# Gathering the x rows for a graph-and-gate kernel one layer earlier, through a DRAM copy in slot order

## The chip, the cores and the metric

The kernel runs on one core of a Trainium2 chip. The metric is the device time of one execution in microseconds; three runs were timed. A lower number is better.

## The reference

The input is x (10000 x 512, float32) and 10000 edges src -> dst, sorted by dst. What is computed, with every weight a 512 x 512 matrix:

```python
h = layernorm(x)
for l in range(3):
    h_neigh = segment_sum(h[src], dst, N) / max(deg, 1)
    rst = relu(h @ W_self[l] + h_neigh @ W_neigh[l] + b[l])
    h = rst / max(norm(rst), 1e-12)
x = x + h
xn = layernorm(layernorm(x)) # the inner one without, the outer one with gain and bias
# 8 experts of width 64; the two with the largest gate count, weighted by their softmax
x = x + layernorm(layernorm(x) + experts(xn)) # with out_g and out_b
```

So the last stage needs, for every node, its row of the input x beside its h of the third layer.

## The kernel before, in words

Edges are cut into T = 79 tiles of 127, and every node gets a slot in one of 79 x 128 = 10112 slots, so that a tile of 128 slots holds the nodes whose edges end there. `pinT` and `poutT` are tables of node numbers by slot. The program has four phases:

- Phase 0 walks over the nodes in natural order (79 tiles): layernorm, then two products (with W_neigh and W_self of layer 0), stored to DRAM as `y_rows0` and `self_rows0`. The weights are prepared and the tables built beside it.
- Phases 1 and 2 walk over the slot tiles. A step gathers the y rows of the edges (`gather`, L670), sums them by slot on TensorE (`aggregate`, L1639 and L1640), adds the node's own row (`combine`, L1295), normalizes (`sum_squares` L1303, `sum_floor` L1313, `norm` L695 on GpSimd, `hhi` L847, `hlo` L1319), turns the tile (L1599, L1172), multiplies it with both matrices of the next layer (`neigh` and `own`, 12 matmuls each, L454), and stores y (`put_y`, L702, an indirect DMA) and the own row (`store_self`, L541).
- Phase 3 aggregates the third layer and runs the residual, the gate and the experts. `x2` (L1338) adds the node's row of x, which `by_node` (L683), an indirect DMA of GpSimd, has gathered into `X[0]` or `X[1]`. `result` (L1499) makes the output tile and `put_out` (L756) scatters it.

Each engine runs its own list in order. `run_tiles` writes these lists: a stage with offset k works in step t on tile t + k. In phase 2 the list of GpSimd (POOL in the profile) for a step is gather(t+6), put_y(t), norm(t+3); that of SyncE (SP), which issues the plain DMAs, is store_self(t), load_self(t+5). In a step of phase 2 VectorE (DVE) does one_hot(t+5), hlo(t+2), ylo(t), turn(t+1), carry_lo, combine, sum_squares and sum_floor of t+3, and `sev` of t (L1189), for which SP's store waits. TensorE (PE) does neigh(t), turn(t+1), own(t), aggregate(t+3). Sl, X and SB are rings of two buffers, so that a load waits for the use of the tile two before, and `after(engine, sem, n)` is that wait.

In phase 1 `by_node` has the same place in the list of POOL and gathers the own rows into Sl; in phase 3 it stands between gather(t+7) and `xob` (L730, x2 plus the output bias, 128x512) and waits for the x2 of the tile before.

Of the kernel before, what the change touches and what calls it, by code (L numbers as in the profile page):

```python
# [14 lines left out]
P = 128  # L15
# [119 lines left out]
class SlotSems:  # L135


    def __init__(self, sem):
        self.g = [sem(f"g{i}") for i in range(GRING)]
        self.x = [sem(f"x{i}") for i in range(2)]  # L140
        self.xs = [sem(f"xs{i}") for i in range(2)]
        self.xg = [sem(f"xg{i}") for i in range(2)]
        self.ys = [sem(f"ys{i}") for i in range(2)]
        self.s2 = [sem(f"s2{i}") for i in range(2)]
        self.smat = sem("smat")
        self.c0 = sem("c0")
        self.chi = sem("chi")
        self.clo = sem("clo")
        self.agg = sem("agg")
        self.r = sem("r")  # L150
        self.rr = sem("relu")
        self.dv2 = sem("sumsq")
        self.ss = sem("sumsq_max")
        self.sc = sem("rnorm")
        self.hhi = sem("hhi")
        self.hlo = sem("hlo")
        self.tr = sem("turned")
        self.ht = sem("ht")
        self.y = sem("y")
        self.yhi = sem("yhi")  # L160
        self.ylo = sem("ylo")
        self.sp = sem("own")
        self.sev = sem("self")
# [54 lines left out]
def build(nc, x, src, dst, W_self, W_neigh, b, Wg, W1, b1, W2, b2, ln_g, ln_b, out_g, out_b, out):  # L218
    with ExitStack() as ctx:
# [9 lines left out]
        def dram(name, shape, dt):  # L229
            return nc.dram_tensor(name, shape, dt)  # L230
# [2 lines left out]
        Yd = [dram(f"y_rows{l}", [N, 2 * D], F16) for l in range(LAYERS)]  # L233
        Sd0 = dram("self_rows0", [N, D], F32)
        Sd = [None] + [dram(f"self_rows{l}", [SLOTS, D], F32) for l in (1, 2)]
        info = dram("node_info", [N, 2], F32)
        table = dram("slot_table", [SLOTS, 2], F32)

# [221 lines left out]
        @block.sync  # L460
        def _(sp):

            sp.wait_ge(s_epad, 3)
            full = (E // EPT) * EPT
            for to, frm, count in ((eDi, dst, E), (eSi, src, E), (eNi, dst[1:E], E - 1)):
                sp.dma_start(to[0:T - 1, :], frm[0:full].rearrange("(t k) -> t k", k=EPT)).then_inc(s_eload, 16)
                sp.dma_start(to[T - 1:T, 0:count - full], frm[full:count].rearrange("(a k) -> a k", a=1)
                             ).then_inc(s_eload, 16)

            sp.wait_ge(s_infoz, 2)  # L470
            sp.dma_start(info.rearrange("(p k) two -> p (k two)", p=NP_), zero).then_inc(s_tinit, 16)
            sp.dma_start(table.rearrange("(p k) two -> p k two", p=T), tinit).then_inc(s_tinit, 16)

            sp.dma_start(bcol[:, :], ln_b.rearrange("(c p) -> p c", p=P)).then_inc(s_bload, 16)
            sp.dma_start(gcol[:, :], ln_g.rearrange("(c p) -> p c", p=P)).then_inc(s_bload, 16)
            for l in range(LAYERS):
                sp.dma_start(bias[:, l, :], b[l, :].partition_broadcast(P)).then_inc(s_bload, 16)
            sp.dma_start(b1b[:, :], b1.rearrange("e h -> (e h)").partition_broadcast(P)).then_inc(s_bload, 16)
            sp.dma_start(ogb[:, :], out_g.partition_broadcast(P)).then_inc(s_bload, 16)
            sp.dma_start(obb[:, :], out_b.partition_broadcast(P)).then_inc(s_bload, 16)  # L480
            sp.dma_start(wgr[:, :, :], Wg.rearrange("(c p) e -> p c e", p=P)).then_inc(s_bload, 16)
            for i in range(3):
                sp.dma_start(b2r[EXPERTS * i:EXPERTS * (i + 1), :], b2[:, :]).then_inc(s_bload, 16)
            def load_weight(m):
                name = NAMES[m]
                if m >= 2:

                    sp.wait_ge(s_wlo, m - 1)
                    sp.wait_ge(s_whi, m - 1)
                to = raw[:, m % 2, :, :]  # L490
                if name == "w1":
                    for c in range(KC):
                        sp.dma_start(to[:, c, :].rearrange("p (e h) -> p e h", e=EXPERTS),
                                     W1[:, c * P:(c + 1) * P, :].rearrange("e p h -> p e h")).then_inc(s_wload[m % 2], 16)
                elif name == "w2":
                    w2f = W2.rearrange("e h d -> (e h) d")
                    for c in range(KC):
                        sp.dma_start(to[:, c, :], w2f[c * P:(c + 1) * P, :]).then_inc(s_wload[m % 2], 16)
                else:
                    w, l = M_OF[name]  # L500
                    for c in range(KC):
                        sp.dma_start(to[:, c, :], w[l, c * P:(c + 1) * P, :]).then_inc(s_wload[m % 2], 16)

            load_weight(0)
            load_weight(1)


            s = ph[0]

            def load_x(t):  # L510

                after(sp, s.rr, (t + -1).n)
                rows = P if not (t.t == TN - 1) else NLAST
                sp.dma_start(X[t.slot(2)][0:rows, :], x[bass.ds(t.t * P, rows), :]).then_inc(s.x[t.slot(2)], 16)

            def store(t):
                rows = P if not (t.t == TN - 1) else NLAST
                sp.wait_ge(s.yhi, (t + 1).n)
                sp.wait_ge(s.ylo, (t + 1).n)
                sp.dma_start(Yd[0][bass.ds(t.t * P, rows), :], YB[t.slot(2)][0:rows, :]).then_inc(s.ys[t.slot(2)], 16)  # L520
                sp.wait_ge(s.sev, (t + 1).n)
                sp.dma_start(Sd0[bass.ds(t.t * P, rows), :], SB[t.slot(2)][0:rows, :]).then_inc(s.s2[t.slot(2)], 16)

            run_plan(TN, [(4, load_x), (0, store)],
                     [(-2, load_weight, 2), (-2, load_weight, 3)]
                     + [(WSTEP(m - 1) + 1, load_weight, m) for m in range(4, len(NAMES))])

            for l in (1, 2):
                s = ph[l]
                q = ph[l - 1]  # L530
                if l == 2:
                    for i in range(2):
                        sp.wait_ge(q.s2[i], 16 * ((T + 1 - i) // 2))

                def load_self(t, s=s, l=l):
                    after(sp, s.r, (t + -1).n)
                    sp.dma_start(Sl[t.slot(2)][:, :], Sd[l - 1][bass.ds(t.t * P, P), :]).then_inc(s.xs[t.slot(2)], 16)

                def store_self(t, s=s, l=l):
                    sp.wait_ge(s.sev, (t + 1).n)  # L540
                    sp.dma_start(Sd[l][bass.ds(t.t * P, P), :], SB[t.slot(2)][:, :]).then_inc(s.s2[t.slot(2)], 16)  # L541

                if l == 1:
                    run_tiles(T, [(0, store_self)])
                else:
                    run_tiles(T, [(0, store_self), (5, load_self)], 1)
            s = ph[3]
            for i in range(2):
                sp.wait_ge(ph[2].s2[i], 2 * 16 * ((T + 1 - i) // 2))

            def load_self3(t):
                after(sp, s.r, (t + -1).n)
                sp.dma_start(Sl[t.slot(2)][:, :], Sd[2][bass.ds(t.t * P, P), :]).then_inc(s.xs[t.slot(2)], 16)

            run_tiles(T, [(6, load_self3)], 2)


        @block.gpsimd
        def _(pool):
# [96 lines left out]
            for l in (1, 2, 3):  # L656
# [17 lines left out]
                def by_node(t, s=s, l=l):  # L674
# [2 lines left out]
                    own = t.own  # L677
                    if l == 1:
                        after(pool, s.r, (t + -1).n)
                    else:  # L680
                        after(pool, f3.x2, (own + -1).n)
                    to, frm = (Sl[i], Sd0) if l == 1 else (X[i], x)
                    pool.indirect_dma_start(to[:, :], None, frm[:, :],  # L683
                                            bass.IndirectOffsetOnAxis(ap=pinT[:, t.t:t.t + 1], axis=0),
# [20 lines left out]

                if l < 3:
                    st = [(6, gather), (0, put_y), (3, norm)]
                    if l == 1:
                        st.append((5, by_node))
                    run_tiles(T, st, l - 1)  # L710
            s = ph[3]

# [39 lines left out]
            def put_out(t):  # L752
# [5 lines left out]
                                        ).then_inc(f3.out[i], 16)  # L758

            run_tiles(T, [(3, rs_of), (4, norm), (-4, zr_of), (-1, hs_of), (-5, put_out), (7, gather),  # L760
                                   (5, by_node), (1, xob)], 2)
            for i in range(2):
                pool.wait_ge(f3.out[i], 16 * ((T + 1 - i) // 2))

# [186 lines left out]
        def _(dve):  # L951
# [379 lines left out]
            def x2(t):  # L1331
                i, q = t.slot(2), t.slot(8)
                dve.wait_ge(s.sc, (t + 1).n)
                dve.wait_ge(s.rr, (t + 1).n)
                t = t.own
                dve.wait_ge(s.xg[i], t.landed(2))
                after(dve, f3.o, (t + -7).n)
                dve.scalar_tensor_tensor(X2[q], RR[i][:, :], scl[:, i:i + 1], X[i][:, :], ALU.mult, ALU.add  # L1338
                                         ).then_inc(f3.x2, 1)
# [391 lines left out]
```

## Time and profile before

| | us |
|---|---|
| median of three runs | 2582.86 |
| the three runs | 2578.65, 2582.86, 2586.2 |
| the profiled execution | 2578.8 |
| its span | 2577.1 |

| engine | busy us | share |
|---|---|---|
| PE | 2199.6 | 85% |
| DVE | 2030.8 | 79% |
| POOL | 1494.3 | 58% |
| ACT | 1067.2 | 41% |

The profiled execution is 1.7 us longer than its span, and 4.1 us below the median. A share is a mean over four phases with different limits: phase 0 lasts to about 600 us, phase 1 to about 1107, phase 2 to about 1622, and phase 3 to the end. The granted clock of TensorE had a mean of 0.945.

### The profile page before, as it was taken

Reading aid. Unit: us, or ns where it says so; the run is one execution under the profiler, and the core shown is the slowest. Engines: PE = TensorE matmul, PEld = TensorE weight load, DVE = VectorE, ACT = ScalarE, POOL = GpSimd, SP = SyncE. Lnnn points to the kernel's source line nnn. Section 1 sums busy time; section 2 is a strip of 40 time slices with the busy share of each in tenths; the row PEclk is TensorE's granted clock in tenths of the full one; section 3 lists DMA queues with packets and bytes.
Section 4 is the critical chain, followed back from the end, with each engine's and each line's share of the span. In section 5 each row is a group of like instructions: output and inputs, shape, how many; then the busy total and the mean of one; then the engine's idle time right before and its main releaser. Section 6 shows DMA issues by size and latency. Waiting matters only on the chain.

```text
span 2577.1 us, 40007 instructions
## 1 busy us (share of the span) xinstructions
PE 2199.6 (85%) x12544; PEld 1022.3 (40%) x12550; DVE 2030.8 (79%) x4940; ACT 1067.2 (41%) x1915; POOL 1494.3 (58%) x1614
## 2 busy tenths in 40 slices
PE   2998898887999999979999999578777878787876
PEld 1444344333444444434444444233333333333333
DVE  4778886565878788758787887598888888888887
ACT  1322111112333333323333333565656565656553
POOL 3751008724555555534444443578888888888875
PEclk9999999998999999989999999798998988988998
DMA  3553337834545555444444444322323232323221
GB/s 120 140 155 114 113 137 117 112 108 127 168 163 168 168 170 164 151 138 168 163 169 171 168 164 151 126 87 85 96 84 97 86 94 87 94 87 95 86 78 40
DMA packets 146407, 322.61 MB, mean 125 GB/s; under 512 B 30769, under 2 KB 30943, under 8 KB 146199
## 3 DMA queue, kind: packets, MB, share of 16 engines
q0 software_dynamic: 55760, 165.43, 20.4%
q1 hardware_dynamic: 90439, 154.63, 20.2%
q8 instruction: 103, 1.69, 0.3%
q14 instruction: 105, 0.86, 0.1%
HBM read 175.76 MB, written 144.83 MB: 124 GB/s over the span
## 4 chain that ended last, share of the span: by engine, by line
DVE 30%; PE 25%; issue 22%; POOL 16%; ACT 5%; DMA 1%; DVEq 0%; POOLq 0%; ACTq 0%
PE psY L454 11%; PE psS L454 10%; DVE R L1295 4%; POOL scl L695 4%; POOL rs L720 4%; POOL slot_table L597 4%; DVE gv L1421 3%; POOL node_info L597 3%; DVE YB L1179 3%; DVE HT L1172 2%; DVE area L1338 2%; ACT HH L847 2%; DVE area L1469 2%; PE psT L1599 2%; DVE HH L1319 2%
## 5 line engine op out<-in xcount | busy, mean ns | idle before, releaser
L454 PE MATMUL psY<-w_n,HT 128*128 128x512 f16 x2844 | 672.1, 387 | 78.9 <-DVE HT L1172 75.6
L454 PE MATMUL psS<-w_s,HT 128*128 128x512 f16 x2844 | 652.5, 379 | 0.0
L454 PEld LDWEIGHTS psY<-w_n,HT 128*128 128x128 f16 x2844 | 265.6, 99 | 471.0 <-DVE HT L1172 170.9
L454 PEld LDWEIGHTS psS<-w_s,HT 128*128 128x128 f16 x2844 | 268.6, 98 | 280.2
L695 POOL TENSOR_TENSOR scl<-ssm,halfpow 128x1 f32<-128x1 f32 x237 | 174.3, 736 | 292.1 <-DVE ssm L1313 292.1
L454 PE MATMUL psS<-w_w,raw 128*128 128x512 f16 x948 | 284.1, 463 | 10.3 <-ACT raw L942 10.3
L702 POOL DMA_INDIRECT y_rows<-YB,poutT x158 | 160.2, 1014 | 188.1 <-DVE YB L1179 161.4
L839 ACT ACTIVATE RR<-R 128x512 f32<-128x512 f32 x237 | 148.2, 625 | 231.6 <-DVE R L1295 231.5
L454 PE MATMUL psY<-w_w,HT 128*128 128x512 f16 x948 | 219.6, 382 | 0.1
L803 ACT ACTIVATE HH<-R 128x512 f16<-128x512 f32 x79 | 49.6, 628 | 369.3 <-DVE R L1160 369.2
L1499 DVE SCALAR_TENSOR_TENSOR raw<-area,zr 128x512 f32<-128x512 f32 x79 | 113.8, 1440 | 101.2 <-issue 98.7
L620 POOL TENSOR_TENSOR scl<-ssm,halfpow 128x1 f32<-128x1 f32 x79 | 44.3, 561 | 252.4 <-DVE ssm L1153 246.7
L1319 DVE SCALAR_TENSOR_TENSOR HH<-RR,scl,HH 128x512 f16<-128x512 f32 x158 | 118.7, 751 | 88.9 <-ACT HH L847 88.9
L1189 DVE SCALAR_TENSOR_TENSOR SB<-psS,downs,bias 128x512 f32<-128x512 f32 x237 | 177.9, 750 | 12.8 <-PE psS L454 10.7
L1179 DVE SCALAR_TENSOR_TENSOR YB<-psY,YB 128x512 f16<-128x512 f32 x237 | 162.0, 683 | 29.0 <-ACT YB L812 29.0
L1295 DVE SCALAR_TENSOR_TENSOR R<-psA,invs,Sl 128x512 f32<-128x512 f32 x237 | 173.2, 731 | 10.4 <-ACT G L828 9.7
L454 PEld LDWEIGHTS psS<-w_w,raw 128*128 128x128 f16 x948 | 109.9, 116 | 175.2 <-issue 95.4
L847 ACT ACTIVATE HH<-RR,scl 128x512 f16<-128x512 f32 x158 | 114.0, 722 | 148.8 <-POOL scl L695 148.8
L1303 DVE SCALAR_TENSOR_TENSOR junk<-R 128x512 f32<-128x512 f32 x237 | 164.2, 693 | 5.5
L1599 PE MATMUL psT<-iden,HH 128*128 128x128 f16 x1896 | 146.7, 221 | 19.8 <-DVE HH L1164 14.5
L1172 DVE COPY HT<-psT 128x1024 f16<-128x1024 f16 x237 | 161.1, 680 | 0.0
L1599 PEld LDWEIGHTS psT<-iden,HH 128*128 128x128 f16 x1896 | 127.6, 99 | 79.0 <-issue 17.7
(266 smaller groups left out, 3946.8 us busy)
## 6 DMA issues: line engine op xcount, KB each, us to landing
self_rows<-SB SPq DMA_DIRECT2D x236, 256.0 KB, 2.0
Sl<-self_rows SPq DMA_DIRECT2D x158, 256.0 KB, 3.0
X<-in_x_dram SPq DMA_DIRECT2D x78, 256.0 KB
y_rows<-YB SPq DMA_DIRECT2D x78, 256.0 KB, 2.3
raw<-in_L_gnn_W_neigh_dram SPq DMA_DIRECT2D x12, 256.0 KB, 4.6
raw<-in_L_gnn_W_self_dram SPq DMA_DIRECT2D x12, 256.0 KB, 4.9
y_rows<-YB,poutT POOLq DMA_INDIRECT x158, 3.0
raw<-in_L_ffn_W_dram SPq DMA_DIRECT2D x8, 256.0 KB, 4.1
```

Source lines behind the costliest of these rows:

```text
L454: mm = eng.matmul(acc, lhs[:, a, c, :], w[:, bpart, c, :], start=(n == 0), stop=(stop and n == 3 * KC - 1))
L597: pool.indirect_dma_start(to[:, :], bass.IndirectOffsetOnAxis(ap=index[0:rows, k:k + 1], axis=0), value[0:rows, k, :], None, bounds_check= ...
L695: pool.tensor_tensor(scl[:, i:i + 1], ssm[:, i:i + 1], halfpow[:, 1:2], ALU.pow).then_inc(s.sc, 1)
L702: pool.indirect_dma_start(Yd[l][:, :], bass.IndirectOffsetOnAxis(ap=poutT[:, t.t:t.t + 1], axis=0), YB[i][:, :], None, bounds_check=node_l ...
L847: act.activation(HH[i][:, 0, :], RR[i][:, :], ACT.Copy, scale=scl[:, i:i + 1]).then_inc(s.hhi, 1)
L1172: dve.tensor_copy(HT[i][:, :, :, :], psT[i][:, :, :, :]).then_inc(s.ht, 1)
L1179: dve.scalar_tensor_tensor(YB[i][:, D:2 * D], psY[i][:, :], k, YB[i][:, 0:D], ALU.mult, ALU.subtract).then_inc(s.ylo, 1)
L1189: dve.scalar_tensor_tensor(SB[i][:, :], psS[i][:, :], downs[:, c:c + 1], bias[:, l, :], ALU.mult, ALU.add).then_inc(s.sev, 1)
L1295: dve.scalar_tensor_tensor(R[i][:, :], psA[0 if l == 3 else i][:, :], invs[:, l - 1, t.t:t.t + 1], Sl[i][:, :], ALU.mult, ALU.add).then_in ...
L1303: dve.scalar_tensor_tensor(junk[:, :], R[i][:, :], 0.0, R[i][:, :], ALU.max, ALU.mult, accum_out=ss[:, i:i + 1]).then_inc(s.dv2, 1)
L1319: dve.scalar_tensor_tensor(HH[i][:, 1, :], RR[i][:, :], scl[:, i:i + 1], HH[i][:, 0, :], ALU.mult, ALU.subtract).then_inc(s.hlo, 1)
L1599: mm = pe.transpose(psT[i][:, a, c, :], HH[i][:, a, c * P:(c + 1) * P], iden16[:, :])
```

## The change

The gather of x by slot moves from phase 3 to phase 2. It goes into the same buffers X; SP stores each tile to a new DRAM tensor `x_by_slot`, and in phase 3 SP reads the tiles back with plain loads. Two semaphores by buffer are new: `xput` (the store has landed) and `xin` (the load has landed).

```diff
+        Xs = dram("x_by_slot", [SLOTS, D], F32)
...
-                    run_tiles(T, [(0, store_self), (5, load_self)], 1)
+                    def store_x(t, s=s):
+                        i, t = t.slot(2), t.own
+                        sp.wait_ge(s.xg[i], t.landed(2))
+                        sp.dma_start(Xs[bass.ds(t.t * P, P), :], X[i][:, :]).then_inc(s.xput[i], 16)
+
+                    run_tiles(T, [(0, store_self), (5, load_self), (3, store_x)], 1)
...
-            run_tiles(T, [(6, load_self3)], 2)
+            for i in range(2):
+                sp.wait_ge(s.xput[i], 16 * ((T + 1 - i) // 2))
+
+            def load_x3(t):
+                t = t.own
+                after(sp, f3.x2, (t + -1).n)
+                sp.dma_start(X[t.slot(2)][:, :], Xs[bass.ds(t.t * P, P), :]).then_inc(s.xin[t.slot(2)], 16)
+
+            run_tiles(T, [(6, load_self3), (5, load_x3)], 2)
...
                     if l == 1:
                         after(pool, s.r, (t + -1).n)
-                    else:
-                        after(pool, f3.x2, (own + -1).n)
+                    elif t.t >= 2:
+                        pool.wait_ge(s.xput[i], (own + -2).landed(2))
...
                     st = [(6, gather), (0, put_y), (3, norm)]
-                    if l == 1:
-                        st.append((5, by_node))
+                    st.append((5, by_node))
                     run_tiles(T, st, l - 1)
...
             run_tiles(T, [(3, rs_of), (4, norm), (-4, zr_of), (-1, hs_of), (-5, put_out), (7, gather),
-                                   (5, by_node), (1, xob)], 2)
+                                   (1, xob)], 2)
...
-                dve.wait_ge(s.xg[i], t.landed(2))
+                dve.wait_ge(s.xin[i], t.landed(2))
```

What this does to the lists of three places follows. First POOL in phase 2, before (L695 is norm, L670 the gather of y, L702 put_y; a word in brackets is the semaphore waited for):

```order
L695 TENSOR_TENSOR scl<-ssm,halfpow 128x1 [waits hlo,sumsq_max]
L670 DMA G<-y_rows,srcT 128x1024 [waits agg]
L702 DMA y_rows<-YB,poutT 10000x1024 [waits ylo,yhi]
L695 TENSOR_TENSOR scl<-ssm,halfpow 128x1 [waits hlo,sumsq_max]
L670 DMA area<-y_rows,srcT 128x1024 [waits agg]
```

And POOL in phase 2 of the changed kernel, where L711 is norm, L699 is by_node, L686 the gather of y and L718 put_y:

```order
L711 TENSOR_TENSOR scl<-ssm,halfpow 128x1 [waits hlo,sumsq_max]
L699 DMA X<-in_x_dram,pinT 128x512 [waits xput1]
L686 DMA G<-y_rows,srcT 128x1024 [waits agg]
L718 DMA y_rows<-YB,poutT 10000x1024 [waits ylo,yhi]
L711 TENSOR_TENSOR scl<-ssm,halfpow 128x1 [waits hlo,sumsq_max]
```

The gather of x, which now waits for a store, stands between one norm and the next, ahead of the other two DMAs. SP in phase 2 of the changed kernel, two steps (L544 is store_self, L540 load_self, L552 store_x; before, the list was the first two alone):

```order
L544 DMA self_rows<-SB 128x512 [waits self]
L540 DMA Sl<-self_rows 128x512 [waits r]
L552 DMA x_by_slot<-X 128x512 [waits xg0]
L544 DMA self_rows<-SB 128x512 [waits self]
L540 DMA Sl<-self_rows 128x512 [waits r]
L552 DMA x_by_slot<-X 128x512 [waits xg1]
```

The store of x is the third transfer of its step, behind a wait for `self`, which is the last instruction of VectorE's step. POOL in phase 3, before (L756 is put_out, L670 the gather of y, L683 by_node, L730 xob, L720 rs_of):

```order
L756 DMA out_0_dram<-raw,poutT 10000x512 [waits f3_o]
L670 DMA area<-y_rows2,srcT 128x1024 [waits agg]
L683 DMA X0<-in_x_dram,pinT 128x512 [waits f3_x2]
L730 TENSOR_TENSOR area<-area,obb 128x512 [waits f3_y]
L720 TENSOR_TENSOR rs<-vv,mhalf2 128x2 [waits f3_r2s,f3_y,f3_v2]
```

And in the changed kernel (L771, L686, L745 and L735 are the same four without by_node):

```order
L771 DMA out_dram<-raw,poutT 10000x512 [waits f3_o]
L686 DMA G<-y_rows,srcT 128x1024 [waits agg]
L745 TENSOR_TENSOR area<-area,obb 128x512 [waits f3_y]
L735 TENSOR_TENSOR rs<-vv,mhalf 128x2 [waits f3_r2s,f3_y,f3_v2]
```

`xob` now follows straight on the gather of y.

## Rows read from the trace of the kernel before

**Rows 1.** Busy time by stretch: us, then PE, PEld, DVE, ACT, POOL, granted clock, DMA share, GB/s
```profile
1300.00:1400.00 100.00, 98.90 (x536) 45.90 (x534) 80.15 (x158) 38.58 (x64) 41.95 (x48) 1.00 0.49 168
2100.00:2200.00 100.00, 79.89 (x500) 36.26 (x498) 87.78 (x249) 61.05 (x121) 82.03 (x87) 0.88 0.28 86
```
**Rows 2.** Timeline of phase 2: start us, us, engine, line, out<-in, [idle before <-releaser]
```profile
1306.07 0.57 POOL L695 TENSOR_TENSOR scl<-ssm,halfpow 128x1 f32<-128x1 f32 x1 [1.75 <-DVE ssm L1313]
...
1308.10 0.68 DVE L1179 SCALAR_TENSOR_TENSOR YB<-psY,YB 128x512 f16<-128x512 f32 x1
...
1308.70 0.68 DVE L1172 COPY HT<-psT 128x1024 f16<-128x1024 f16 x1
...
1309.43 2.76 PE L454 MATMUL psY<-w_n,HT 128*128 128x512 f16 x12
...
1309.57 1.02 POOL L702 DMA_INDIRECT y_rows<-YB,poutT  x1 [1.68 <-DVE YB L1179]
1310.08 0.68 DVE L1280 SCALAR_TENSOR_TENSOR G<-psA,G 1x512 f16<-1x512 f32 x1 [0.70 <-ACT G L828]
...
1312.27 0.75 DVE L1189 SCALAR_TENSOR_TENSOR SB<-psS,downs,bias 128x512 f32<-128x512 f32 x1
```
**Rows 3.** Timeline of phase 2, SP's queue alone
```profile
1300.46 0.32 SPq L541 DMA_DIRECT2D self_rows<-SB  x1
1300.83 0.43 SPq L537 DMA_DIRECT2D Sl<-self_rows  x1
...
1319.30 0.32 SPq L541 DMA_DIRECT2D self_rows<-SB  x1
```
**Rows 4.** Timeline of phase 1, POOL alone
```profile
904.68 1.07 POOL L683 DMA_INDIRECT Sl<-self_rows,pinT  x1 [0.19 <-issue]
...
907.41 1.01 POOL L702 DMA_INDIRECT y_rows<-YB,poutT  x1 [0.35 <-issue]
```
**Rows 5.** DMAs of 1200 to 1600 us: queue row, issues with median us to landing
```profile
q1 hardware_dynamic: 18432, 33.56, 26.3%
...
self_rows<-SB SPq DMA_DIRECT2D x64, 256.0 KB, 2.0
Sl<-self_rows SPq DMA_DIRECT2D x64, 256.0 KB, 2.8
```
**Rows 6.** DMAs of 1700 to 2500 us, in phase 3
```profile
X<-in_x_dram,pinT POOLq DMA_INDIRECT x68, 4.5
```
**Rows 7.** Timeline of a steady step of phase 3
```profile
2011.18 1.47 DVE L1499 SCALAR_TENSOR_TENSOR raw<-area,zr 128x512 f32<-128x512 f32 x1 [1.37 <-issue]
...
2013.95 1.04 POOL L670 DMA_INDIRECT area<-y_rows,srcT  x1 [0.31 <-issue]
...
2015.22 0.68 DVE L1303 SCALAR_TENSOR_TENSOR junk<-R 128x512 f32<-128x512 f32 x1
...
2016.68 1.42 DVE L1421 SCALAR_TENSOR_TENSOR gv<-iota_row,gv 128x8 f32<-128x8 f32 x1
2016.81 1.27 POOL L730 TENSOR_TENSOR area<-area,obb 128x512 f32<-128x512 f32 x1
...
2019.04 1.24 POOL L720 TENSOR_TENSOR rs<-vv,mhalf 128x2 f32<-128x2 f32 x1 [0.97 <-DVE vv L1369]
```
**Rows 8.** Line L1421, 1700 to 2500 us: ns min/median/max, first and last start
```profile
L1421 DVE SCALAR_TENSOR_TENSOR gv<-iota_row,gv x69: 209/1427/1446, 1701.8 to 2497.6; 128x8 f32<-128x8 f32 x69
```
**Rows 9.** Timeline of an early step of phase 3
```profile
1669.46 2.02 DVE L1406 CAST gv<-gi 128x2 f32<-128x2 uint32 x1
1670.17 1.28 POOL L730 TENSOR_TENSOR area<-area,obb 128x512 f32<-128x512 f32 x1
1671.39 0.68 DVE L1303 SCALAR_TENSOR_TENSOR junk<-R 128x512 f32<-128x512 f32 x1
```
**Rows 10.** Timeline of the second tile of phase 3
```profile
1641.06 0.75 DVE L1338 SCALAR_TENSOR_TENSOR area<-RR,scl,X 128x512 f32<-128x512 f32 x1 [2.14 <-DMA X<-in_x_dram,pinT]
```
**Rows 11.** Timeline of phase 3: matmuls at the lower clock
```profile
1999.51 3.18 PE L454 MATMUL psS<-w_w,raw 128*128 128x512 f16 x7
```

More of the change, by code:

```diff
@@ L142, in __init__ @@
         self.xg = [sem(f"xg{i}") for i in range(2)]
+        self.xput = [sem(f"xput{i}") for i in range(2)]
+        self.xin = [sem(f"xin{i}") for i in range(2)]
         self.ys = [sem(f"ys{i}") for i in range(2)]
```

## The prediction

> **What bounds the kernel now.** I read the table of busy time by stretch first, because the change touches two phases with different limits. In phase 2 TensorE is busy 98.9% of the time at a granted clock of 1.00 (2.4 GHz), and POOL only 42%; in phase 3 no engine is full, DVE 88%, POOL 82% and TensorE 80% [rows 1]. So the change takes work from a phase in which POOL looks loaded and puts it where POOL looks idle. Whether that helps depends on what waits for POOL, so I went on to the timelines.
>
> *Phase 2.* The reader is to see a loop that is just closed. POOL's norm starts at 1306.07; DVE's turn copy, which needs its result through ACT and two more DVE instructions, runs at 1308.70, and TensorE's next `neigh` starts at 1309.43, right behind it [rows 2]. From the start of a norm to the start of that `neigh` are 3.36 us with no slack in them. TensorE then needs a whole step, and DVE's `sev` of that step is last: SP's store at 1319.30 [rows 3] puts the end of `sev` at 1319.27, that is 9.84 us after the `neigh`. The step is (1319.30 - 1300.46) / 3 = 6.28 us. TensorE is busy 6.21 of it, so any delay of the norm beyond some hundredths comes out as time.
>
> *Phase 3.* The step is (2497.6 - 1701.8) / 68 = 11.70 us [rows 8]. POOL waits 0.97 us for DVE's vv just before `rs_of` (L720), and DVE waits 1.37 us before `result` (L1499), which needs POOL's zr [rows 7]. The loop is POOL's rs_of, norm and zr, then DVE from `result` to vv. POOL's other work, put_out, gather, by_node and xob, lies in the shadow of the DVE part: after xob POOL still waits 0.97 us. Taking by_node from there makes the wait longer and nothing else, except through one thing. The tiny L1421 (128x8) takes 1.42 us because it runs against xob: it starts at 2016.68 and ends at 2018.10, just when xob (2016.81 + 1.27) is over [rows 7]. Elsewhere the same instruction took 0.21 us; the median is 1.43 [rows 8]. That collision is on the loop.
>
> **The change part by part.**
>
> *Phase 2, SP.* `sev` of step t ends at 1300.43 (call it S). SP issues store_self at S + 0.03 and load_self at S + 0.40, which takes 0.43 us [rows 3]; so store_x (of tile t+3) is issued at S + 0.88. Its own wait, for a gather issued two steps ago, is long over: such gathers land in 4.5 us [rows 6], a step is over 6.
>
> *Its landing.* The trace has no third 256 KB transfer in a row. The first of the step lands in 2.0 us and the second, issued 0.37 later, in 2.8 [rows 5]. The queue moved 128 transfers in 26.3% of 400 us, so one takes 0.82 us of all 16 engines [rows 5]. The third thus lies 0.82 - 0.45 = 0.37 above the second: 3.2 us. Ends: 2.0 if it overlaps freely, 4.5, the slowest 256 KB row, if the two transfers that phase 2 gets per step crowd it [rows 6].
>
> *Phase 2, POOL.* by_node(t+5) waits for that landing, and behind it in the list stand gather(t+7), put_y(t+1) and norm(t+4). For the release I put 0.1 us, an estimate between nothing and the 0.31 us that POOL needs between two DMAs [rows 7]. In phase 1, where the three DMAs stand in the same order with a wait that is already over, they take from 904.68 to 908.42, 3.74 us [rows 4]. So norm(t+4) starts at S + 0.88 + 3.2 + 0.1 + 3.74 + 0.03 = S + 7.95. Before, it started at 1306.07 = S + 5.64. The idle 58% of POOL doesn't help, because the wait is in front of the norm.
>
> *The new step.* Round the loop: sev, store, by_node, norm(t+4), neigh(t+3), sev(t+3) is 7.95 + 3.36 + 9.84 = 21.15 us for three steps, 7.05 each. A second loop goes through DVE alone: from a norm to the end of its turn copy are 3.31 us; from there to the end of sev (1313.02) 3.64, of which DVE idled 0.70 before the carry at 1310.08 [rows 2], so 2.94 remain, and 7.95 + 3.31 + 2.94 = 14.20 for two steps is 7.10. The two agree. (Check on before: 5.64 + 3.36 + 9.84 = 18.84 = 3 x 6.28.) I take 7.07, +0.79 us a step. by_node waits in 77 tiles: **+61 us**. With a landing of 2.0 the step is (6.75 + 13.2) / 3 = 6.65 and the cost +28 us; with 4.5 the second loop decides, (9.25 + 6.25) / 2 = 7.75, and it is +113.
>
> A sentence apart: the Trainium skill (DMA: Bandwidth & Descriptors, Anatomy of one DMA) gives a fixed cost of about 2.0 us plus the bytes over 436 GB/s. By it the store would land in an estimated 2.6 us, the step would be 6.85 and this term +44 us; the trace has 2.0 for a lone store and 2.8 behind one, so the queue is what the page leaves out, and I stay with the rows.
>
> *A lock on POOL's DMAs.* put_y starts at 1309.57, 0.19 us after the end of a DVE turn copy, though its input YB was ready at 1308.78 [rows 2]. In the new step the copy ends near S + 4.2, about where by_node is released. If it is held, it costs 0.2 to 0.3 us a loop, +5 to +8 us in all; I leave it in the range. If it happens in every step the sum below becomes 2629 to 2632. [...]
>
> *Start of phase 2.* Two x gathers slip in between the first y gathers, 1.35 us each, while POOL has slack; +1 us (0 to 3).
>
> *Phase 3, POOL.* by_node goes, and with it the 1.82 us from the gather's end (2013.95 + 1.04 = 2014.99) to xob's start (2016.81). xob then starts straight behind the gather, near 2015.02, and ends at 2016.30. There it meets DVE's sum_squares (L1303), which started at 2015.22 [rows 7]. That is the very picture of the early steps: there a CAST of DVE stood from 1669.46, xob ran from 1670.17 to 1671.45, and L1303 started at 1671.39, 0.06 before xob's end [rows 9]. So L1303 will start at 2016.24, 1.02 late, and L1421 later saves 1.43 - 0.21 = 1.22. Net -0.20 us a step. The steps that collide are some 72 (69 in the 800 us shown): **-14 us**. Bounds: nothing, if another DVE instruction is held as well; -88 us, if L1303 goes free.
>
> *Phase 3, SP.* One load more per step in a queue that has one. load_x3(t+5) is issued beside load_self and needed two steps (23 us) later; even 4.5 us [rows 6] are hidden. If the cover were gone the price would be the landing, but nothing shortens 23 us. At the start, x2 of the second tile waited 2.14 us for the gather of X [rows 10]; SP's loads come at once. Part of it is behind the norm anyway: -2 us (0 to -4).
>
> *Sum.* 2578.8 + 61 + 1 - 14 - 2 = 2624 us against the profiled execution. The median of the runs is 4 us higher; I say 2625.
>
> **Rivals.**
>
> A. *The collision in phase 3 is simply gone.* xob lands on DVE instructions that don't mind it, and each step gives 1.22 us: -88, and with the store at its fast end (+28) the time is 2578.8 - 88 + 28 + 1 - 2 = 2518; with +61 it is 2551. For it: DVE instructions that read PSUM ran beside xob unharmed. Against it: in the early steps it was L1303 that came out behind xob.
>
> B. *The store is hidden.* If it landed before the norm is due, phase 2 would not change, and 2578.8 - 14 - 2 = 2563. That needs a landing of 5.64 - 0.88 - 0.1 - 3.74 - 0.03 = 0.9 us; the fastest store has 2.0 [rows 5]. Only an error of mine about which tile's store is waited for would bring it.
>
> C. *The clock falls in phase 2.* With a step of 7.07 TensorE idles 0.86 us before each `neigh`, where it had hardly any. In phase 3 it falls: 7 matmuls took 3.18 us [rows 11], 12 would take 5.2 instead of 2.76. If every `neigh` ran so, the loop of three steps would get 2.4 us longer, 0.8 a step, +62: 2686. Against it: the lower clock in phase 3 follows gaps of over 3 us; this gap is below 1.
>
> D. *The change does nothing*, as its lists would show; they show the gather moved.
>
> **How the numbers follow.** A difference of 0.3% (8 us) is about what a measurement of this kernel can tell from none. Forecast 0.77; A 0.10; B 0.05; C 0.08. The forecast's own range is 2590 (landing 2.0, a little more from phase 3) to 2680 (landing near 4.2). A and B lie below, C just above; leaving them out leaves out about 2 in 10, so the range is 2585 to 2680. Faster: A and B, less a tenth where A is slowed, 0.13. Same: the low edge of the forecast, 0.04. Slower: 0.83.
>
> **What would show it.** In phase 2 the step should go from 6.28 to about 7.07 us, TensorE's share from 99% to near 88%, and a new row should stand among the waits: POOL's by_node for the DMA of x_by_slot, 2 to 3 us in nearly each of 77 tiles. The store's landing should read 3.2 us, and norm should no longer be released by DVE's ssm. In phase 3 L1421 should take 0.2 us, L1303 or the CAST before it be stretched by over 1 us, and the step be 11.5. If phase 2 keeps its 6.28 the loop is wrong; if phase 3 goes below 11 the collision is.

## The result, and the profile after

The changed kernel takes 2704.62 us (median of 4 runs, 2701.51 to 2706.52) against 2583.56 us before. The ratio is 1.047, 95% interval 1.0450 to 1.0489: slower, by 121 us where I forecast about 45. The profiled execution has a span of 2704.5 us against 2577.1.

The rows of after that answer to [rows 1], same columns:

```profile
1300.00:1400.00 100.00, 82.87 (x431) 38.14 (x432) 63.61 (x128) 29.05 (x49) 48.23 (x50) 0.95 0.60 190
2100.00:2200.00 100.00, 78.96 (x506) 36.23 (x505) 87.69 (x253) 62.60 (x124) 70.21 (x80) 0.91 0.29 92
```

In phase 2 TensorE fell from 98.9% busy to 83%; phase 3 hardly changed, but POOL has 12 points less to do there. The waits of 1200 to 1600 us say who waits for whom (us in total, times, longest):

```profile
POOL X L699 <- DMA x_by_slot<-X: 176.2, 48, 5.7
ACT HH L862 <- POOL scl L711: 158.2, 50, 5.4
DVE HH L1334 <- ACT HH L862: 136.2, 50, 5.0
```

POOL waits 3.7 us for the store in nearly every step (48 times in 400 us), and norm, ACT and VectorE follow it one after the other. Before, norm waited for DVE's ssm [rows 2]. The chain in one step of the timeline, where L544, L540 and L552 are SP's three transfers, L699 is by_node, L718 put_y and L711 norm:

```profile
1409.04 0.32 SPq L544 DMA_DIRECT2D self_rows<-SB  x1
1409.40 0.43 SPq L540 DMA_DIRECT2D Sl<-self_rows  x1
1409.88 0.74 SPq L552 DMA_DIRECT2D x_by_slot<-X  x1
...
1413.94 1.07 POOL L699 DMA_INDIRECT X<-in_x_dram,pinT  x1 [4.25 <-DMA x_by_slot<-X]
...
1416.62 1.01 POOL L718 DMA_INDIRECT y_rows<-YB,poutT  x1 [0.30 <-issue]
1417.67 0.57 POOL L711 TENSOR_TENSOR scl<-ssm,halfpow 128x1 f32<-128x1 f32 x1
```

The order is the one that I had drawn from [rows 2 to 4]. From the end of sev (1409.01) to norm are 8.66 us here, and 9.65 in the mean of the 66 steps between 1150 and 1700 us; I had put 7.95. The step follows from the first and last norm (ns min/median/max, first and last start):

```profile
L711 POOL TENSOR_TENSOR scl<-ssm,halfpow x68: 567/589/639, 1150.6 to 1693.1; 128x1 f32<-128x1 f32 x68
```

(1693.1 - 1150.6) / 67 = 8.10 us, where I forecast 7.07; before it was 6.30 between the same kind of rows. The store's landing, which answers to [rows 5], is the last figure of the second row (DMAs of 1250 to 1600 us):

```profile
Sl<-self_rows SPq DMA_DIRECT2D x43, 256.0 KB, 4.1
x_by_slot<-X SPq DMA_DIRECT2D x43, 256.0 KB, 4.6
```

In phase 3 (answering to [rows 7, 8]) xob is L745, the CAST L1421, sum_squares L1318 and the 128x8 instruction L1436:

```profile
2110.42 1.27 POOL L745 TENSOR_TENSOR area<-area,obb 128x512 f32<-128x512 f32 x1
...
2110.55 1.18 DVE L1421 CAST gv<-gi 128x2 f32<-128x2 uint32 x1
...
2111.64 0.68 DVE L1318 SCALAR_TENSOR_TENSOR junk<-R 128x512 f32<-128x512 f32 x1
...
2113.11 0.21 DVE L1436 SCALAR_TENSOR_TENSOR gv<-iota_row,gv 128x8 f32<-128x8 f32 x1
```

The collision moved as forecast, from the 128x8 instruction to the CAST. The row of L1436 gives the step, (2596.9 - 1906.0) / 60 = 11.51 us against 11.70:

```profile
L1436 DVE SCALAR_TENSOR_TENSOR gv<-iota_row,gv x61: 207/213/216, 1906.0 to 2596.9; 128x8 f32<-128x8 f32 x61
```

The two phases account for the spans: 77 steps of phase 2 by 1.80 are +139 us, 72 of phase 3 by -0.19 are -14, together +125 of +127.

### The profile page after: what moved, and what is told of

The parts are those of the page before. It is cut to its first block and busy times, and to the rows that moved or that the text cites. A ratio compares the mean times of both kernels' runs of the same rounds, so it can differ in the third digit from the quotient of the medians.

```text
span 2704.5 us, 40172 instructions
## 1 busy us (share of the span) xinstructions
PE 2242.7 (83%) x12550; PEld 1032.2 (38%) x12550; DVE 2011.7 (74%) x4940; ACT 1063.6 (39%) x1915; POOL 1480.9 (55%) x1614
## 5 line engine op out<-in xcount | busy, mean ns | idle before, releaser
L457 PE MATMUL psY<-w_n,HT 128*128 128x512 f16 x2844 | 709.1, 403 | 179.4 <-DVE HT L1187 171.0
L457 PEld LDWEIGHTS psY<-w_n,HT 128*128 128x128 f16 x2844 | 275.0, 102 | 598.0 <-DVE HT L1187 262.3
L711 POOL TENSOR_TENSOR scl<-ssm,halfpow 128x1 f32<-128x1 f32 x237 | 177.5, 749 | 153.8 <-DVE ssm L1328 152.0
L699 POOL DMA_INDIRECT X<-in_x_dram,pinT x79 | 89.2, 1129 | 278.3 <-DMA x_by_slot<-X 271.7
L718 POOL DMA_INDIRECT y_rows<-YB,poutT x158 | 162.2, 1027 | 84.1 <-issue 50.1
L735 POOL TENSOR_TENSOR rs<-vv,mhalf 128x2 f32<-128x2 f32 x79 | 94.8, 1200 | 206.0 <-DVE vv L1384 206.0
L1318 DVE SCALAR_TENSOR_TENSOR junk<-R 128x512 f32<-128x512 f32 x237 | 164.2, 693 | 5.5
```

Source lines behind the costliest of these rows:

```text
L457: mm = eng.matmul(acc, lhs[:, a, c, :], w[:, bpart, c, :], start=(n == 0), stop=(stop and n == 3 * KC - 1))
L711: pool.tensor_tensor(scl[:, i:i + 1], ssm[:, i:i + 1], halfpow[:, 1:2], ALU.pow).then_inc(s.sc, 1)
L718: pool.indirect_dma_start(Yd[l][:, :], bass.IndirectOffsetOnAxis(ap=poutT[:, t.t:t.t + 1], axis=0), YB[i][:, :], None, bounds_check=node_l ...
L735: pool.tensor_tensor(rs[:, i, :], vv[:, i, :], mhalf2[:, :], ALU.pow).then_inc(f3.rs, 1)
L1318: dve.scalar_tensor_tensor(junk[:, :], R[i][:, :], 0.0, R[i][:, :], ALU.max, ALU.mult, accum_out=ss[:, i:i + 1]).then_inc(s.dv2, 1)
```

## The experiments

Theory 1 was the loop: sev, store, landing, by_node, norm, and round again. The rivals were the traffic (six transfers a step for four) and POOL's extra work.

**Store first.** The store keeps everything but its place in SP's list.

```diff
-                    run_tiles(T, [(0, store_self), (5, load_self), (3, store_x)], 1)
+                    run_tiles(T, [(3, store_x), (0, store_self), (5, load_self)], 1)
```

> The changed kernel with one thing moved: SP's store of the x tile stands first in its step, ahead of the wait for VectorE's sev, instead of third. Same transfers, same work on POOL. Theory 1 (a latency loop: POOL's gather of x waits for a store that was issued only after sev): the store is issued about one step earlier and has landed when POOL asks; norm starts again 5.6 us after the end of sev instead of 9.65, the step of phase 2 is 6.3 to 6.5 us (8.10 now), the wait of POOL for x_by_slot is gone, and the time is about 2568 us (2560 to 2590). Theory 2 (the traffic, 6 transfers of 256 KB a step instead of 4, is what costs): the step stays near 8.1 and the time near 2705. Theory 3 (POOL's own 1.4 us more per step in front of the norm): also near 2705, the norm then follows the DMAs without any wait.

Measured: 2570.18 us, ratio to before 0.9954 (0.9942 to 0.9966). The stretch in phase 2 and the norm's row:

```profile
1300.00:1400.00 100.00, 97.24 (x540) 46.01 (x538) 79.32 (x159) 38.62 (x64) 57.29 (x64) 1.00 0.74 249
```

```profile
L711 POOL TENSOR_TENSOR scl<-ssm,halfpow x70: 554/564/602, 1152.4 to 1587.3; 128x1 f32<-128x1 f32 x70
```

The step is 6.30 us again, with POOL busier (57%) than in the change as made (48%), and the DMA engines too (0.74, 249 GB/s; the change as made 0.60, 190 GB/s; before 0.49, 168). So in phase 2 neither the traffic nor POOL's work costs anything that shows; the wait does. This version also beats the kernel before, by 12 us or 0.5%: small, but clear of the noise.

The moment of the store hardly moves by this edit. SP, once past load_self, goes straight on to the store of its next step, so that it is still issued 0.87 us behind a sev, third in the row. What is new is the tile: it now stores the one that POOL asks for a step later.

**Gather one tile later.** The same step of distance from the other end: POOL asks later for the same store.

```diff
-                    st.append((5, by_node))
+                    st.append((5 if l == 1 else 4, by_node))
```

> The changed kernel with POOL's gather of x working on tile t+4 in step t instead of t+5; its place in POOL's list and the store's place in SP's queue (third, behind the wait for sev) stay. Now the gather asks for a store issued a whole step earlier. Theory 1 (the loop sev, store, landing, gather, norm): a step of slack covers the landing of 4.9 us, the step of phase 2 is 6.3 and the time about 2570 us. Rival (the store itself is too late behind sev, or three transfers behind each other on SP hold up the load of Sl): the time stays above 2600.

Measured: 2572.88 us, ratio 0.9948 (0.9934 to 0.9961). The norms run from 1149.9 to 1584.4 in 69 steps, 6.30 each. The store is still third and still behind sev, which is harmless as long as nobody asks for it in the same step.

**The two halves.** Phase 2's half keeps by_node in phase 3 as well; phase 3's half has no gather or store of x in phase 2, and loads plain tiles of x in natural order in phase 3.

```diff
-            run_tiles(T, [(6, load_self3), (5, load_x3)], 2)
+            run_tiles(T, [(6, load_self3)], 2)
...
-                                   (1, xob)], 2)
+                                   (5, by_node), (1, xob)], 2)
```

> Only the half of the change in phase 2: x is gathered and stored there as in the changed kernel, but phase 3 gathers its x rows itself, as before. All theories: phase 2 has a step of 8.1 us, phase 3 one of 11.70, and the time is 2584 + 139 = 2723 us (2712 to 2735). If the two halves interact, it comes out elsewhere.

Measured: 2714.99 us (one run), 133 above the 2582.24 of before beside it. The two rows are the norm in phase 2 and the 128x8 instruction in phase 3:

```profile
L714 POOL TENSOR_TENSOR scl<-ssm,halfpow x66: 573/585/615, 1156.1 to 1682.3; 128x1 f32<-128x1 f32 x66
```

```profile
L1441 DVE SCALAR_TENSOR_TENSOR gv<-iota_row,gv x47: 207/1431/1448, 1906.1 to 2445.1; 128x8 f32<-128x8 f32 x47
```

Steps of 8.10 and 11.72 us, the first as after and the second as before, with the 1.43 us instruction.

Phase 3's half:

```diff
-                sp.dma_start(X[t.slot(2)][:, :], Xs[bass.ds(t.t * P, P), :]).then_inc(s.xin[t.slot(2)], 16)
+                sp.dma_start(X[t.slot(2)][:, :], x[bass.ds(min(t.t * P, N - P), P), :]).then_inc(s.xin[t.slot(2)], 16)
...
-                    run_tiles(T, [(0, store_self), (5, load_self), (3, store_x)], 1)
+                    run_tiles(T, [(0, store_self), (5, load_self)], 1)
...
-                    st.append((5, by_node))
+                    if l == 1:
+                        st.append((5, by_node))
```

> Only the half in phase 3: no gather and no store of x in phase 2; phase 3 loads tiles of x with plain loads, in natural order in place of slot order (so the values of x at this point are those of other nodes). Expected: phase 2 has its step of 6.28, phase 3 one of 11.51 instead of 11.70, since the 128x8 instruction no longer runs against xob but the CAST does; the time is 2584 - 14 - 2 = 2568 us (2562 to 2576). The rival (the gain of phase 3 is larger, because taking the gather out also frees something that the changed kernel's slow phase 2 hid): under 2560.

Measured: 2569.39 us, ratio 0.9952 (0.9938 to 0.9966), 13 us faster than before beside it. It is as fast as the whole change with the store first (2570.18, with the same runs of before beside it). So the change has nothing to gain but these 13 us, and the gather and the store of x are free in phase 2 once nobody waits. The halves add up: +133 - 13 = +120, measured +121.

**Store second.** Ahead of load_self, behind sev.

```diff
-                    run_tiles(T, [(0, store_self), (5, load_self), (3, store_x)], 1)
+                    run_tiles(T, [(0, store_self), (3, store_x), (5, load_self)], 1)
```

> The changed kernel with the store of x second in SP's step, ahead of load_self but still behind the wait for sev. It is issued 0.48 us earlier. If its landing (4.8 us) is set by the place in SP's queue, it also lands 0.5 us sooner, the step of phase 2 falls by (0.48 + 0.5) / 2 = 0.5 to 7.6 and the time is 2705 - 38 = 2667 us. If the landing is set by POOL's gathers and scatters that are in flight at that moment, only the 0.48 count: step 7.86, time 2687 us.

Measured: 2653.86 us, ratio 1.0276 (1.0260 to 1.0293). From issue to by_node are 4.19 us in the mean (4.90 as third), so one place further ahead in SP's row brings the landing 0.7 us nearer, more than the 0.5 expected, beside the 0.48 us of the earlier issue. The step is 7.51, and the time is below both cases (2667 and 2687).

**Wait without the gather.** by_node only waits; SP no longer waits for the gather's data.

```diff
                     elif t.t >= 2:
                         pool.wait_ge(s.xput[i], (own + -2).landed(2))
+                    if l == 2:
+                        return
...
-                        sp.wait_ge(s.xg[i], t.landed(2))
```

> The changed kernel without the gather of x itself: POOL still waits at the same place for the store of tile t+3, and SP stores what stands in the buffer (so x_by_slot doesn't hold the x rows). POOL's part behind the wait is shorter by one DMA, 1.37 us (3.88 to 2.5). If the landing (4.9 us) is set by all transfers in flight, one of six less takes some 0.8 us off it: from sev to norm 9.65 - 1.37 - 0.8 = 7.5 us, step (7.5 + 6.25) / 2 = 6.9, time 2705 - 93 = 2612 us. If the landing is set by SP's own three alone, 4.9 stays: 8.3, step 7.3, time 2643. If the wait doesn't matter and POOL's work does, the step falls by 1.37 to 6.7 and the time to 2597.

Measured: 2640.97 us (one run), against 2643 for SP's own queue, 2612 for all transfers in flight and 2597 for POOL's work alone. From issue to POOL's next DMA are 4.47 us, 0.43 less than with the gather. That lies midway between the first two cases (nothing and 0.8 us less). The time is close to the first alone because the sum behind all three cases leaves out the 0.12 to 0.15 us a step that every measured step has on top (see the table below). The step is 7.25. POOL's work as the whole cost is refuted.

**Half the store.** 128 KB instead of 256; phase 3 loads plain rows of x.

```diff
-                        sp.dma_start(Xs[bass.ds(t.t * P, P), :], X[i][:, :]).then_inc(s.xput[i], 16)
+                        sp.dma_start(Xs[bass.ds(t.t * P, P), 0:D // 2], X[i][:, 0:D // 2]).then_inc(s.xput[i], 16)
```

> The changed kernel with only the first half of each x row stored (128 KB instead of 256), and phase 3 loading plain tiles of x in place of x_by_slot (values of other nodes). If the landing goes with the bytes in flight, it is 0.4 us shorter, the step 0.2 us, the time 2705 - 16 = 2689 us. If it is a fixed time of a store, nothing moves: 2705. If the traffic of phase 2 were the limit, 11 of 12 parts of it: step 7.4, 2653.

Measured: 2689.27 us, ratio 1.0396 (1.0380 to 1.0411). The time falls by 15 us, as the case of the bytes in flight has it (16). The landing is less clear: its median falls from 4.6 to 4.2 us, but from issue to by_node the mean falls only from 4.90 to 4.76, and the profiled execution (2697.98 us, a step of 7.97) was the slowest of the four. A landing that doesn't depend on the bytes, and traffic as the limit (2653), are refuted; the share of the bytes is not measured well.

**The same wait where POOL has slack.** This is the kernel without the gather, with the wait in front of put_y.

```diff
-                    elif t.t >= 2:
-                        pool.wait_ge(s.xput[i], (own + -2).landed(2))
...
                     pool.wait_ge(s.ylo, (t + 1).n)
+                    if l == 2 and t.t + 2 < T:
+                        pool.wait_ge(s.xput[i], (t.own + 2).landed(2))
```

> As the kernel without the gather of x (POOL does not gather x in phase 2, SP stores what stands in X, so x_by_slot does not hold the x rows), but the wait for the same store, third in SP's queue, now stands in front of put_y instead of in front of the gather of y. POOL has 2 to 3 us of slack there. This measures the landing in a kernel whose step has not grown, with POOL's gather of y issued 0.15 us after sev and nothing of POOL before it. If the landing is set by the place in SP's queue (my sum: 3.2 us), put_y starts at sev + 4.2 and the norm is not held: step 6.28, time 2570. If the third transfer takes 4.5 or more in any case, put_y ends at sev + 6.5, the norm comes 0.9 us late, and step and time are 6.7 and 2600. If a wait on POOL costs whatever its slack, the time is near the 2641 of the other kernel.

Measured: 2609.57 us (one run), the second case. Landings by the profile, here (first row, DMAs of 1200 to 1550 us) and in the kernel of *Wait without the gather*, where the wait is ahead of the gather of y (second row, 1250 to 1600 us):

```profile
x_by_slot<-X SPq DMA_DIRECT2D x53, 256.0 KB, 4.0
```

```profile
x_by_slot<-X SPq DMA_DIRECT2D x49, 256.0 KB, 4.1
```

Here POOL moves only what it moved before the change, the gather of y and put_y. Both overlap the store: the gather is mostly issued within 1 us of it, ahead or behind, and put_y of the step before, issued 2.0 us ahead of the store in the mean, was still in flight in 25 of 27 steps whose landing the trace has. With this traffic the third transfer already takes 4.0 us, not 3.2. put_y starts 4.74 us behind the store's issue in the mean, so the norm comes at sev + 6.79 and the step is 6.78. The price of the wait is what is left after its slack: POOL waits longer here than in the change as made, 3.8 us a step (195.9 us in 52 times), and loses 0.5 us a step instead of 1.8.

**Two versions for phase 3**, both on the kernel with the store first. First xob is put ahead of the gather of y:

```diff
-            run_tiles(T, [(3, rs_of), (4, norm), (-4, zr_of), (-1, hs_of), (-5, put_out), (7, gather),
-                                   (1, xob)], 2)
+            run_tiles(T, [(3, rs_of), (4, norm), (-4, zr_of), (-1, hs_of), (-5, put_out), (1, xob),
+                                   (7, gather)], 2)
```

> The kernel with the store of x first in SP's step (2570 us), and in phase 3 POOL's xob ahead of the gather of y instead of behind it. xob then runs beside VectorE's bn_stats and combine, which it did not hold up so far. If only xob held the CAST (1.19 us), it is free: about 1.0 us a step less, 2570 - 75 = 2495 us. If a DMA of POOL holds the CAST too (as the CAST of 2.02 us in the early steps of the kernel before suggests), the gather takes xob's place and the gain is 0.1 to 0.2 us a step: 2555 to 2562.

Measured: 2636.97 us, ratio 1.0202 (1.0186 to 1.0218), 67 us above the kernel with the store first where a gain was expected. L771 is put_out, L1353 x2, L745 xob:

```profile
2056.30 1.37 POOL L771 DMA_INDIRECT out_dram<-raw,poutT  x1 [0.17 <-issue]
...
2056.81 2.73 DVE L1353 SCALAR_TENSOR_TENSOR area<-RR,scl,X 128x512 f32<-128x512 f32 x1
2057.70 1.28 POOL L745 TENSOR_TENSOR area<-area,obb 128x512 f32<-128x512 f32 x1
```

x2, with both operands in SBUF, starts while POOL makes put_out's DMA, and ends only 0.56 us after xob. In the change as made x2 starts beside the same put_out and takes 0.75 us in all 48 steps looked at; the difference is that a DMA follows there and not xob. The CAST is free (0.16 us), but 2 us are lost for 1 won.

Then VectorE's zf, which reads PSUM, is put where xob runs:

```diff
-                (3, x2_mean_var), (-1, gap), (-1, index_float), (4, lambda t: sum_squares(t, 3)), (-1, first_hot),
-                (3, x2_eps), (-4, zf), (-1, both_hot), (3, x2_inverse),
+                (3, x2_mean_var), (-1, gap), (-4, zf), (-1, index_float), (4, lambda t: sum_squares(t, 3)), (-1, first_hot),
+                (3, x2_eps), (-1, both_hot), (3, x2_inverse),
```

> The kernel with the store of x first (2570 us), and on VectorE in phase 3 zf (L1484, 0.74 us, which reads PSUM) moved from behind both stages that xob holds up to just before the CAST. If only instructions of VectorE with both operands in SBUF (and the CAST) are held by xob, zf runs beside xob, the CAST starts 0.66 us later and is held 0.4 us instead of 1.03: the step of phase 3 falls from 11.51 to 10.85 and the time to 2570 - 50 = 2520 us (2512 to 2530). If the hold just moves on to another instruction, or the matmuls for zf are not done that early, nothing is gained: 2570 or more.

Measured: 2531.55 us, ratio 0.9792 (0.9776 to 0.9808), the fastest kernel of the study, 54 us under the 2586.05 of before beside it. Against the kernel with the store first it gains 39 us, or 42 by the two ratios to before, where 50 were expected; 2531.55 is just above the stated 2512 to 2530. The L1484 row is zf:

```profile
2104.89 1.29 POOL L745 TENSOR_TENSOR area<-area,obb 128x512 f32<-128x512 f32 x1
...
2105.02 0.74 DVE L1484 SCALAR_TENSOR_TENSOR area<-psS,downs,area 128x512 f32<-128x512 f32 x1
2105.68 0.54 DVE L1421 CAST gv<-gi 128x2 f32<-128x2 uint32 x1
```

zf runs beside xob at its full speed (0.74 to 0.75 us in all 50 steps looked at), the CAST is held 0.4 us, and the next row gives a step of (2447.6 - 1910.4) / 49 = 10.96 us, 0.1 above what was expected:

```profile
L1436 DVE SCALAR_TENSOR_TENSOR gv<-iota_row,gv x50: 225/227/228, 1910.4 to 2447.6; 128x8 f32<-128x8 f32 x50
```

## Why the prediction was wrong

The direction and the path of the wait were right; one term, the store's landing with its release, was too small, and with it the sum. By its own steps:

- *Where the wait stands.* Right. One step more of distance between the store and its wait, from either end (2570.18, 2572.88), gives the whole loss back, with the same transfers and the same work of POOL.
- *Its landing.* This is the step that failed. I took 2.8 us for the second transfer of a step, added 0.37 for the third and wrote 3.2, plus 0.1 until by_node starts: 3.3. Measured: 4.90 from issue to by_node, of which the landing is 4.6 and the start 0.3. The 0.37 came from 0.82 us of engine time per transfer; that was true as a mean of the queue, but I added it as if the third transfer had nothing beside it but its own row. In the kernel with the wait at put_y, where POOL has the traffic that it had before the change, the second transfer already takes 3.4 us in place of 2.8 and the third 4.0. With the gather of x beside it, as in the change, it is 4.6. That this last 0.6 us is the one transfer more was not shown: in the versions with the store first all six transfers are there as well, and the store lands in 4.2 us. The row is of the last version above, DMAs of 1250 to 1600 us:

```profile
x_by_slot<-X SPq DMA_DIRECT2D x55, 256.0 KB, 4.2
```

  So the order of POOL's DMAs around the store matters too; how much is due to SP's row, to the gather and to this order stays open. The sentence on the Trainium skill gave 2.6 us; that fit (DMA: Bandwidth & Descriptors, Anatomy of one DMA) is given for DMAs that GpSimd issues, and the store is SP's. The fastest third transfer of 256 KB in these traces took 3.0 us.
- *The lock on POOL's DMAs.* It didn't come, and my reading of [rows 2] was wrong. by_node starts 0.27 or 0.28 us behind the landing in 65 of 66 steps, also where VectorE's turn copy still runs. put_y starts 0.78 to 0.80 us behind its YB in all 67 steps looked at before the change, and 0.80 to 0.82 us behind the landing in all 62 steps with the wait at put_y. So the 0.79 us are put_y's own start, whatever releases it, and the 0.19 us behind the copy only tell where the copy stands in VectorE's list.
- *POOL behind the wait.* 3.88 us in the mean against 3.74, nearly right.
- *The loops.* The kernels tell how well the formula carries. With D for the time from the end of sev to norm, and the constants 6.25 and 13.2 of the prediction's two loops, the greater of (D + 6.25) / 2 and (D + 13.2) / 3 decides:

| kernel | D, measured | step by the loops | step measured |
|---|---|---|---|
| the change | 9.65 | 7.95 | 8.10 |
| half the store | 9.44 | 7.85 | 7.97 |
| store second | 8.48 | 7.37 | 7.51 |
| wait, no gather | 7.95 | 7.10 | 7.25 |
| wait at put_y | 6.79 | 6.66 | 6.78 |

It is 0.12 to 0.15 us low in each of the five. With D = 9.65 instead of 7.95 my +61 us become +129; the constant 0.15 adds 11, and the sum is 140 against +139 measured. What the 0.12 to 0.15 are stays open. Landings vary from step to step (3.4 to 6.8 us after the change), and of two loops that nearly tie the later one counts each time, which a formula of means leaves out; I did not test it. The clock is hardly it (see below).
- *The range.* A landing near 4.2 gives +102 us and a time of 2665 by my own sum, so 2680 already held something for the lock and for the 4 us between the profiled execution and the median. The 4.5 that I had written down as an end gives 2677 (2689 with the open 0.15 us a step), still below the 2705 measured: by_node started 4.90 us behind the issue, above every 256 KB row that I had taken for a bound. The sum itself is 2624.8, and with the 4 us 2629, not 2625.
- *Phase 3.* Right: 11.51 us forecast as 11.5, L1421's 1.43 us gone, the CAST at 1.19 in its place, -13 us measured by the half alone. The 72 steps of -0.19 us account for that by themselves; the -2 that I had for the start doesn't show.
- *The clock.* I gave it a case of its own, and set it aside because TensorE would idle only 0.86 us before a `neigh`, while in phase 3 the lower clock followed gaps of over 3 us. Part of it came. The idle time before a `neigh` is 1.5 us in the mean, the granted clock in phase 2 is 0.95 or below in place of 1.00, and 19 of 66 `neigh` groups took 4.1 to 4.5 us for 2.76, which is 0.47 us a step in the mean. The gaps before those 19 were 2.0 to 3.6 us, and a gap of 3.50 was also followed by a `neigh` at the full clock:

```profile
1406.21 2.76 PE L457 MATMUL psY<-w_n,HT 128*128 128x512 f16 x12 [3.50 <-DVE HT L1187]
1421.03 4.45 PE L457 MATMUL psY<-w_n,HT 128*128 128x512 f16 x12 [2.31 <-DVE HT L1187]
```

  What of the change's time this makes was not measured apart. It can only be in the 0.15 us that the formula is low for the change, and hardly there: with the wait at put_y only 1 of 65 groups was slow, 0.03 us a step in the mean, and the formula is 0.12 us low all the same.
- *The rivals.* A, the collision simply gone, is refuted by the step of 11.51 us and the CAST at 1.19. The larger gain in phase 3, which I added before the experiments, is refuted by the half alone, and B, *the hidden store*, by the wait itself.

## What to carry to other kernels

Before a gather or load is put into an idle engine's list, look at what its wait is for and who stands behind it. An idle engine hides work, but not a wait in front of something that is on a loop. One step more of distance between a store and whoever waits for it, by its place in the queue or by the tile it asks for, cost nothing here and was worth 134 us. The landing of the first or second transfer of a step said too little about the third: a loop that passes through a landing should be priced from a row with as many transfers in flight as the new step has, or with a range that admits there is none. And where one engine held another, it paid to put an instruction that isn't held beside it (39 us won), while moving the holder lost 67 us.

## What was not expected of the hardware

- The third of three 256 KB transfers issued 0.4 us apart landed in 4.0 to 4.6 us where the first took 2.1, though the 16 engines were busy only 60% of the time over the phase. At 74% (store first) it landed in 4.2, and nothing was late, since nobody asked in the same step.
- put_y, an indirect DMA that scatters, started 0.79 us after its last input was ready, or 0.80 us after a landing; the two gathers started 0.27 to 0.28 us after a landing in nearly all steps.
- Three instructions of VectorE with all operands in SBUF, issued while POOL made a DMA, were held until the POOL tensor instruction behind that DMA was over: 2.73 us instead of 0.75 for x2, 1.43 instead of 0.21 for the 128x8 instruction, 2.02 instead of 0.16 for the CAST [rows 9]. With another DMA behind, the same x2 beside the same put_out took 0.75 us. zf, which reads PSUM, ran beside xob at its full speed.
